# Second mixer's output stage: the corrected product made token-major, head statistics along the columns

## The reference

```python
y = y.transpose(1, 0, 2, 3).reshape(Bx, Tx, C)
yg = y.reshape(Bx, Tx, H, HS)
mu = yg.mean(-1, keepdims=True)
var = ((yg - mu) ** 2).mean(-1, keepdims=True)
y = ((yg - mu) / jnp.sqrt(var + EPS)).reshape(Bx, Tx, C) * ln_w + ln_b
rk = (r.reshape(Bx, Tx, H, HS) * k.reshape(Bx, Tx, H, HS) * time_faaaa.reshape(H, HS)).sum(-1, keepdims=True)
y = y + (rk * v.reshape(Bx, Tx, H, HS)).reshape(Bx, Tx, C)
return y * g @ Wo.T
...
x = _layernorm(x + _L0_attn_ref(...))
x = _layernorm(x + _L0_ffn_ref(...))
x = _layernorm(x + _L1_attn_ref(...))
x = _layernorm(x + _L1_ffn_ref(...))
```

## Time and profile before

| | us |
|---|---|
| median of 3 runs | 5771.28 |
| profiled execution, its own time | 5775.05 |
| its span | 5773.2 |
| `wkv_outputs`, first to last instruction | 262.2 (4557.67 to 4819.88) |
| PE busy in it | 200.1 |
| DVE, ACT, POOL busy in it | 117.6, 40.9, 34.9 |

### The profile page before, as it was taken

How to read it: one execution, slowest core, us unless ns; L and a number is a source line. 1 busy time by engine, 2 the same in 40 slices (tenths; PEclk the granted TensorE clock), 3 DMA queues, 4 the chain that set the end, 5 groups by cost and what they waited for, 6 DMA issues and landing times. The chain is left out here.

```text
span 5773.2 us, 105253 instructions
## 1 busy us (share of the span) xinstructions
PE 5136.3 (89%) x36890; PEld 3594.2 (62%) x36890; DVE 3784.4 (66%) x8870; ACT 2786.2 (48%) x6575; POOL 2260.3 (39%) x1588
## 2 busy tenths in 40 slices
PE   5999999999899999999989989995578787998998
PEld 3776776767677677776766646652146675664665
DVE  5656656566565665656658848845699736875884
ACT  1444444444344444444438838844400113883882
POOL 2424334243232433424337717713422114762761
PEclk7999999999999999999989989997699757998998
DMA  3000000000000000000010000000000000000000
GB/s 110 5 7 7 4 7 5 5 7 4 9 4 7 7 4 7 5 5 7 4 32 1 0 27 1 0 7 0 0 8 1 1 1 28 0 18 10 0 0 15
DMA packets 170268, 53.55 MB, mean 9 GB/s; under 512 B 142225, under 2 KB 166161, under 8 KB 169233
## 3 DMA queue, kind: packets, MB, share of 16 engines
q1 hardware_dynamic: 168736, 49.54, 3.7%
q10 hardware_dynamic: 1392, 2.20, 0.1%
HBM read 41.21 MB, written 10.49 MB: 9 GB/s over the span
## 5 line engine op out<-in xcount | busy, mean ns | idle before, releaser
L342 PE MATMUL gd_ps<-gd_taps,gd_xwin 128*128 128x512 f32 x2048 | 907.3, 598 | 8.0 <-ACT gd_qT L528 8.0
L342 PEld LDWEIGHTS gd_ps<-gd_taps,gd_xwin 128*128 128x128 f32 x2048 | 382.7, 191 | 465.5 <-issue 446.0
L787 POOL TENSOR_TENSOR gd_o_rn<-gd_tmp,gd_mhalf 128x8 f32<-128x8 f32 x64 | 103.5, 1635 | 1193.6 <-DVE gd_tmp L706 1193.6
L551 ACT ACTIVATE gd_X<-gd_ps 128x512 f32<-128x512 f32 x512 | 268.2, 633 | 541.6 <-PE gd_ps L384 541.6
L1298 ACT ACTIVATE L_ffn_s<-L_ffn_s,L_ffn_nb,L_ffn_r 128x128 f32<-128x128 f32 x1024 | 419.4, 482 | 3.1
L683 DVE TENSOR_TENSOR gd_Z<-gd_ps,cst 128x256 f32<-128x256 f32 x384 | 163.0, 425 | 327.0 <-PE gd_ps L422 261.0
L1118 POOL TENSOR_TENSOR L_ffn_t<-L_ffn_t 128x512 f32<-128x512 f32 x128 | 190.3, 1487 | 394.3 <-DVE L_ffn_t L1339 394.3
L781 POOL TENSOR_TENSOR gd_gate<-gd_gate,gd_norm_w 128x2048 f32<-128x2048 f32 x32 | 145.0, 4531 | 483.4 <-ACT gd_gate L516 483.4
L384 PE MATMUL gd_ps<-cst,gd_gV 128*128 128x128 f32 x2048 | 264.9, 278 | 53.8 <-DMA gd_gV<-gd_inverses 29.5
L384 PEld LDWEIGHTS gd_ps<-cst,gd_gV 128*128 128x128 f32 x2048 | 225.8, 143 | 77.5 <-ACT gd_decay L546 74.8
L516 ACT ACTIVATE gd_v<-gd_ps 128x512 f32<-128x512 f32 x128 | 76.4, 597 | 406.2 <-PE gd_ps L342 406.2
(11 more groups left out here) (376 smaller groups left out, 13405.1 us busy)
## 6 DMA issues: line engine op xcount, KB each, us to landing
L_ffn_sb_rope<-in_rope SPq DMA_DIRECT2D x4, 2048.0 KB, 8.2
gd_tap_row<-in_L_attn_conv_v SPq DMA_DIRECT2D x2, 2048.0 KB, 7.1
gd_blocks<-gd_nA SPq DMA_DIRECT2D x256, 16.0 KB, 1.7
gd_Z<-gd_blocks SPq DMA_DIRECT2D x32, 128.0 KB, 2.0
gd_inverses<-gd_Z SPq DMA_DIRECT2D x32, 128.0 KB, 1.7
gd_gV<-gd_inverses SPq DMA_DIRECT2D x256, 16.0 KB, 1.9
L_ffn_sb_wqkv<-in_L_ffn_wqkv SPq DMA_DIRECT2D x4, 768.0 KB, 8.7
gd_tap_row<-in_L_attn_conv_q SPq DMA_DIRECT2D x1, 2048.0 KB, 15.4
```

The source lines that it names most:

```text
L342: ins = pe.matmul(ps[4 + i % 2][:], xwin[:, t:t + P] if i < 8 else xwin[:, PAD:PAD + P], taps[:, t, 512 * SLICE[i]:512 * (SLICE[i] + 1)] i ...
L551: act.activation(heads(X, gi).rearrange("p h x -> p (h x)"), ps[4 + gi][:], ACT.Copy).then_inc(x_s.sem, 1)
```

## The change

The product is formed the other way round. For each chunk the 32 tokens of `a` are the weights and `S0x` is streamed, 128 columns, so that tokens come out on the partitions; four chunks fill the 128 partitions of one quarter of the PSUM bank. The part of y from the zero state (`u4`) is added by PE as well, a matmul of its 32 tokens by the identity into the same place. So `corrected` becomes 4 quarters a sequence, of 8 matmuls each, one quarter a step from j = 4 to 11. A head's 8 features now lie next to each other along the free dimension: sum and sum of squares are DVE reductions (512 to 64 columns), root and reciprocal are taken of 64 columns, and `mean` and `variance` are gone from PE. The normalised y is turned back by four transposes (`turn_back`), then bonus, gate, `project` and residual follow feature-major as before, with `yc` as a new buffer. The steps that come last for group k - 1 move into group k + 1: `turn_back` of sequence 1 (j = 0), `project` (j = 1 and 4), the residuals. The loops run over NBLK + 2 rounds.

```diff
...
-        y, ysq = [sb(f"y{b}", [P, FW]) for b in range(B)], [sb(f"ysq{b}", [P, FW]) for b in range(B)]
+        y, ysq, yc = ([sb(f"{n}{b}", [P, FW]) for b in range(B)] for n in ("y", "ysq", "yc"))
+        mu, sd = ([sb(f"{n}{b}", [P, QUARTERS * RH]) for b in range(B)] for n in ("mu", "sd"))
...
+                def normed(k, b):
+                    if not inside(k):
+                        return
                     n = nth(k, b)
+                    dve.wait_ge(yc_mm, QUARTERS * (n + 1))
+                    dve.tensor_reduce(mu[b][:], by_head(ps_y[b][:]), AX_X, ALU.add).then_inc(mu_s, 1)
+                    dve.wait_ge(mu_s, n + 1)
+                    if k:
+                        dve.wait_ge(yb_mm, nth(k - 1, b) + 1)
+                    dve.scalar_tensor_tensor(by_head(y[b][:]), per_head(mu[b][:]), -1.0 / RS, by_head(ps_y[b][:]), ALU.mult, ALU.add).then_inc(cen_s, 1)
+                    dve.wait_ge(sq_s, n + 1)
+                    dve.tensor_reduce(sd[b][:], by_head(ysq[b][:]), AX_X, ALU.add).then_inc(var_s, 1)
                     dve.wait_ge(sd_s, n + 1)
-                    dve.reciprocal(ysq[b][:], ysq[b][:]).then_inc(inv_s, 1)
+                    dve.reciprocal(sd[b][:], sd[b][:]).then_inc(inv_s, 1)
                     dve.wait_ge(inv_s, n + 1)
-                    dve.tensor_tensor(y[b][:], y[b][:], ysq[b][:], ALU.mult).then_inc(nrm_s, 1)
-                    dve.wait_ge(nrm_s, n + 1)
-                    dve.scalar_tensor_tensor(by_chunk(y[b][:]), by_chunk(y[b][:]), lnv[:, 0:1], n4[:, b, chunks(k)], ALU.mult, ALU.add).then_inc(bon_s, 1)
+                    dve.tensor_tensor(by_head(y[b][:]), by_head(y[b][:]), per_head(sd[b][:]), ALU.mult).then_inc(nrm_s, 1)
+
+                def gated(k, b):
+                    if not inside(k):
+                        return
+                    n = nth(k, b)
+                    dve.wait_ge(yb_mm, n + 1)
+                    dve.scalar_tensor_tensor(by_chunk(yc[b][:]), by_chunk(ps_m[b][:]), lnv[:, 0:1], n4[:, b, chunks(k)], ALU.mult, ALU.add).then_inc(bon_s, 1)
                     dve.wait_ge(bon_s, n + 1)
-                    dve.scalar_tensor_tensor(by_chunk(y[b][:]), by_chunk(y[b][:]), lnv[:, 1:2], g4[:, b, chunks(k)], ALU.add, ALU.mult).then_inc(g_s, 1)
+                    dve.scalar_tensor_tensor(by_chunk(yc[b][:]), by_chunk(yc[b][:]), lnv[:, 1:2], g4[:, b, chunks(k)], ALU.add, ALU.mult).then_inc(g_s, 1)
...
-                spread_M(0)
-                for k in range(NBLK):
-                    if k + 1 < NBLK:
-                        spread_M(k + 1)
-                    if k:
-                        finishing(k - 1)
-                finishing(NBLK - 1)
+                spread_M(0, 0)
+                spread_M(0, 1)
+                for k in range(NBLK + 2):
+                    spread_M(k + 1, 0)
+                    gated(k - 2, 1)
+                    spread_M(k + 1, 1)
+                    residual(k - 2, 0)
+                    residual(k - 2, 1)
+                    normed(k - 1, 0)
+                    normed(k - 1, 1)
+                    gated(k - 1, 0)
...
-                def corrected(k, b):
-                    pe.wait_ge(x_s, nth(k, b) + 1)
-                    if k:
-                        pe.wait_ge(sum_s, nth(k - 1, b) + 1)
-                    for j in range(BLK):
-                        ins = pe.matmul(ps_y[b][:, CS * j:CS * (j + 1)], S0x[b][:, j].rearrange("p h i -> p (h i)"), a4[:, b, BLK * k + j], start=True, stop=True)
+                def corrected(k, b, q):
+                    if not inside(k):
+                        return
+                    if q == 0:
+                        pe.wait_ge(x_s, nth(k, b) + 1)
+                        if k:
+                            pe.wait_ge(cen_s, nth(k - 1, b) + 1)
+                    for i in range(BLK // QUARTERS):
+                        j = BLK // QUARTERS * q + i
+                        out = ps_y[b][CS * i:CS * (i + 1), P * q:P * (q + 1)]
+                        pe.matmul(out, u4[:, b, BLK * k + j], ident, start=True, stop=False)
+                        ins = pe.matmul(out, a4[:, b, BLK * k + j], S0x[b][:, j].rearrange("p h i -> p (h i)"), start=False, stop=True)
                     ins.then_inc(yc_mm, 1)
-                def mean(k, b):
-                    pe.wait_ge(sum_s, nth(k, b) + 1)
+                def turn_back(k, b):
+                    if not inside(k):
+                        return
+                    pe.wait_ge(nrm_s, nth(k, b) + 1)
                     if k:
                         pe.wait_ge(out_s, nth(k - 1, b) + 1)
-                    pe.matmul(ps_m[b][:], headsum, y[b][:], start=True, stop=True).then_inc(mean_mm, 1)
-
-                def variance(k, b):
-                    pe.wait_ge(sq_s, nth(k, b) + 1)
-                    pe.matmul(ps_m[b][:], headsum, ysq[b][:], start=True, stop=True).then_inc(var_mm, 1)
+                    for q in range(QUARTERS):
+                        ins = pe.transpose(ps_m[b][:, P * q:P * (q + 1)], y[b][:, P * q:P * (q + 1)], ident)
+                    ins.then_inc(yb_mm, 1)
...
-                for k in range(NBLK):
+                for k in range(NBLK + 2):
                     for j in range(BLK):
                         if BLK * k + j < CB - 1:
                             advance(k, j)
                         if k + 1 < NBLK and j % 2 == 1:
                             turn(k + 1, j // 2)
-                        if k and j in (5, 6):
-                            corrected(k - 1, j - 5)
-                        if k and j in (7, 8):
-                            mean(k - 1, j - 7)
-                        if k and j in (10, 11):
-                            variance(k - 1, j - 10)
-                        if k and j in (14, 15):
-                            project(k - 1, j - 14)
-                for b in range(B):
-                    corrected(NBLK - 1, b)
-                for b in range(B):
-                    mean(NBLK - 1, b)
-                for b in range(B):
-                    variance(NBLK - 1, b)
-                for b in range(B):
-                    project(NBLK - 1, b)
+                        if j == 0:
+                            turn_back(k - 2, 1)
+                        if j == 1:
+                            project(k - 2, 0)
+                        if j == 4:
+                            project(k - 2, 1)
+                        if 4 <= j < 12:
+                            corrected(k - 1, j // 4 - 1, j % 4)
+                        if j == 12:
+                            turn_back(k - 1, 0)
...
                         if k + 1 < NBLK and j % 2 == 1:
                             turned(k + 1, j // 2)
-                        if k and j in (8, 9):
-                            squares(k - 1, j - 8)
-                        if k and j in (11, 12):
-                            root(k - 1, j - 11)
-                for b in range(B):
-                    squares(NBLK - 1, b)
-                for b in range(B):
-                    root(NBLK - 1, b)
+                        if j in (9, 13):
+                            squares(k - 1, j // 13)
+                        if j in (10, 14):
+                            root(k - 1, j // 14)
```

More of the change, by code:

```diff
@@ L1637 @@
 NBLK = CB // BLK
+QUARTERS = 4
 STEP = (CS + 1) * CB
@@ L2091, in wkv_outputs @@
         st_mm, st_s, x_s, yc_mm = (sems("wo_" + n) for n in ("state_mm", "state", "state_spread", "y_mm"))
-        sum_s, mean_mm, cen_s, sq_s, var_mm, sd_s = (sems("wo_" + n) for n in ("y", "mean_mm", "centred", "squares", "var_mm", "root"))
-        inv_s, nrm_s, bon_s, g_s, o_mm, out_s = (sems("wo_" + n) for n in ("inverse", "normed", "bonus", "gated", "out_mm", "out"))
+        mu_s, cen_s, sq_s, var_s, sd_s = (sems("wo_" + n) for n in ("sums", "centred", "squares", "square_sums", "root"))
+        inv_s, nrm_s, yb_mm, bon_s, g_s, o_mm, out_s = (sems("wo_" + n) for n in ("inverse", "normed", "y_turned", "bonus", "gated", "out_mm", "out"))
         a4 = fA[:, 0:B * T].rearrange("p (b t c) -> p b c t", b=B, c=CB)
@@ L2200, in project @@
                 def project(k, b):
+                    if not inside(k):
+                        return
                     pe.wait_ge(g_s, nth(k, b) + 1)
-                    pe.matmul(ps_m[b][:], WoT, y[b][:], start=True, stop=True).then_inc(o_mm, 1)
+                    pe.matmul(ps_m[b][:], WoT, yc[b][:], start=True, stop=True).then_inc(o_mm, 1)
                 for g in range(8):
                     turn(0, g)
-                for k in range(NBLK):
+                for k in range(NBLK + 2):
```

41 lines of the change are left out of this document (16 added, 25 removed).

## The result

Before 5772.8 us, after 5714.4 us (medians of four runs each, 5764.0 to 5775.0 and 5708.4 to 5718.4), ratio 0.990 [0.988, 0.992]. In a later set of runs the changed kernel took 5716.6, ratio 0.990 [0.989, 0.992]. Forecast: 5716. The number is right. The way to it is not: two steps were wrong and nearly cancelled.

What follows compares the result with a forecast made beforehand. PE, busy 200.1 of the stage's 262.2 us at mean clock 0.53, was taken to lead, with waits at boundaries. Three groups and tail: -8.9 - 17.1 - 19.4 - 10.2 = -55.6, giving 5716; range 5693 to 5783.

Steps and rivals of the forecast that it cites:

- Quarter: Eight matmuls of `corrected` on PE: 2.98 us at the lower clock level, 1.6 at the upper, mode changes included.
- I let the last of each run beside the first of the next chunk: 13 passes' time: Overlap of chunks within a quarter: 16 passes take 13 passes' time, 2.78 us lower, 1.39 upper.
- The rival with "two at a time": Quarter in 8 passes' time, 1.71 us lower, 0.86 upper: 5696, or 5739 with the clock low; chance 0.16.
- Change between whole array and strips: PE switching tiling mode around a quarter: about 0.1 us each, twice, 0.2 a quarter.
- Clock: PE's clock in the stage: well above 0.53, 1.00 from the second quarter to the group's end.
- I expect the rise after the first quarter: In each group, clock rises after first quarter, advance and turn, 5.1 us, and stays up to the boundary.
- unit costs: PE at the lower level: pass 0.21 us, advance 1.28, turn or `turn_back` 0.86, 512-column matmul 1.7.
- Boundaries: From POOL's start to the first quarter: 22.1 us into group 2, 16.1 into group 3; group 1's front 18.1.
- Statistics on DVE: Reductions 0.69 us, reciprocal 0.42, beside PE's quarters in the body, costing nothing there.
- Tail: After the last POOL start, to the last residual: 37.9 us, against 48.1 before.
- mark for being wrong: Wrong if clock stays 0.50 through quarters, a quarter exceeds 2 us upper, or ACT holds advances over 1 us a group.
- low-clock rivals: Clock stays low in the stage: 5773 with quarters as costed, chance 0.14; 5739 with chunks two at a time, 0.06.

Runs made afterwards that it cites:

- one, two and four-strip kernels: Changed kernel with a quarter's four chunks on one column strip (5726.6 us), on two (5701.7), or on four, the changed kernel itself (5714.4).
- first trace: First profiled execution of the changed kernel, nothing altered: 5715.4 us in total, 193.0 us in the stage.
- pairs: Changed kernel, chunks issued in another order so a quarter's four lie on two column strips, each landing at its own place: 5705.6 us, ratio to before 0.9889.
- two strips: Changed kernel with a quarter's four chunks on two column strips in turn, chunk order not the reference's: 5701.7 us, ratio to before 0.9886.
- second execution: Another profiled execution of the same changed kernel, nothing altered: 5718.2 us in total, 205.8 us in the stage.

## Why the prediction came out right, step by step

- **Quarter: wrong, in the term "I let the last of each run beside the first of the next chunk: 13 passes' time".** It is 4 passes' time. 1.11 and 0.70 us stand against 2.98 and 1.6. The rule that the forecast weighed (the Trainium skill, TensorE: Matmul & The Clock Gate, Part 3: matmuls on different column strips start and end in program order) gives the 13; the one, two and four-strip kernels speak against it for this case, and so do the rows above, in which passes begin out of program order; the measurement decides. The rival with "two at a time" was nearer and still too dear.
- **Change between whole array and strips: 0.2 forecast, about 0.3 found** (the fixed part of the three strip kernels; in the tail, with no change between quarters, it is gone: 3.4 us for eight). A fixed cost at the change agrees with what the Trainium skill says of a change of tiling mode, that it drains the engine (TensorEngine Tiling (Array Packing), Key Properties).
- **Clock: wrong in five of six cases, and in the sixth not for the reason given.** "I expect the rise after the first quarter" held for group 2 in the first trace, where it came and stayed. But it came 1.6 us after the quarter's start and not behind 5.1 us of quarter, advance and turn, and the clock had risen once before any quarter. The forecast failed in groups 1 and 3 in both traces and in group 2 in the second. That the light quarter is the cause is likely (2 rises in 16 groups against 11 in 13) and not shown: pairs, with the same weight as two strips, rose only in two groups of three. What decides a single group stays open.
- **How they cancel.** The forecast's own unit costs with a quarter of 1.11 and a low clock give bodies of 26.8 us (8 x 1.11 + 12.8 + 4.3 + 0.86) and 22.5, so groups of 44.9, 48.9, 38.6 and a tail of 28.2 (12.7 + 3.4 + 12.1): 61.9 less than before. The forecast had 55.6, the second execution 56.4. Measured bodies were 28.0 and 23.6. A dear quarter at a high clock and a cheap one at a low clock cost about the same. That they do is luck: nothing in the forecast's working ties the two errors together in this way, and the first execution, with one group at the high clock, had 69.2.
- **Boundaries: right** to 1.2 us. DVE's two held instructions, M behind them and PE's wait of 5.8 are as forecast; group 2's first quarter came at +20.9 and, with the clock low, at +22.0 (22.1), group 3's at +16.5 (16.1). Group 1's is off: it came at +16.2 and not at 18.1, since `corrected` now begins at j = 4, where it had begun at 5, and the forecast kept the old place.
- **Statistics on DVE: right**; the reduction is 0.69, the reciprocal 0.55 (0.42). ACT's squares and root did not hold the advances: PE was never idle in group 1's body (28.03 of 28.03 us) and for 0.5 us in group 2's.
- **Tail: 7 us too long in the forecast.** Eight quarters took 3.4 us (4737.06 to 4740.5), not 13.1. Behind them DVE, which does both sequences one after the other, ends 14.6 us later, not 12.1. The interval was 30.7 and 31.4, not 37.9.
- **The mark for being wrong** that the forecast set, a clock of 0.50 through the quarters, is what happened in most groups. The low-clock rivals stood at 5773 and 5739 only because they kept a quarter of 13 or 8 passes' time.

## What to carry to other kernels

Price a new form of matmul from both sides, and carry the price into every step that leans on it: here one wrong price went into the work, the clock and the tail. Moving work into the next group pays only when the engine that feeds it has a short chain; otherwise the wait goes one place on (15.4 us for M instead of 10.2 for the gated product). Judge a stage's gain by at least two traces: one group of the same kernel took 38.2 and 50.1 us.
